# Two spreads of reciprocal sums per tile: from behind the transposes to behind the value products, one frame later

## The reference

```
x = x + 0.5 * ffn(layernorm(x))
x = x + attn(layernorm(x))
x = x + 0.5 * ffn(layernorm(x))
```

```
h = rmsnorm(x);  q, k, v = h @ qkv_w + qkv_b      # 16 query heads, 4 key heads, 64 wide; rotary
attn[h] = exp(q k' / 8 - logaddexp(logsumexp(q k' / 8), sink[h]))     # causal, window 128
x = x + concat_h(attn[h] @ v) @ proj_w + proj_b
h2 = rmsnorm(x);  4 of 32 experts per token by h2 @ gate_w;  x + sum_k w_k * expert_k(h2)
```

## Time and profile before

| | us |
|---|---|
| median of 3 runs (1331.86 to 1332.47) | 1332.41 |
| the profiled execution | 1331.51 |
| its span, first to last instruction | 1329.6 |
| TensorE busy (share of the span) | 1012.1 (76%) |
| VectorE busy | 827.7 (62%) |
| GpSimd busy | 649.6 (49%) |
| ScalarE busy | 565.6 (43%) |

### The profile page before, as it was taken

The page is one execution under the profiler, slowest core; times in us unless marked ns, Lnnn a source line. Parts: engine busy times, 40 slices in busy tenths (PEclk is TensorE's granted clock), DMA queues, the critical chain, the costliest instruction groups (busy, mean ns, idle before and its releaser), DMA issues.

```text
span 1329.6 us, 24766 instructions
## 1 busy us (share of the span) xinstructions
PE 1012.1 (76%) x7773; PEld 733.2 (55%) x7834; DVE 827.7 (62%) x2064; ACT 565.6 (43%) x2156; POOL 649.6 (49%) x860
## 2 busy tenths in 40 slices
PE   2899999999358854888888959999999990888100
PEld 1567666676347743555555536667666660777100
DVE  4788888886324422777777758898888761343121
ACT  0455555556223421555555616555555650444000
POOL 2234565564756225556553232466555545740575
PEclk9899999999769985899999979999999995899655
DMA  6677777766124320000000011233211101442221
GB/s 187 160 177 183 189 193 183 173 165 144 48 80 138 109 70 20 19 17 19 21 17 7 1 40 56 74 103 102 93 57 43 36 17 32 134 125 84 71 67 51
DMA packets 98779, 116.60 MB, mean 88 GB/s; under 512 B 14816, under 2 KB 73952, under 8 KB 98656
## 3 DMA queue, kind: packets, MB, share of 16 engines
q1 hardware_dynamic: 76688, 57.73, 13.8%
q10 hardware_dynamic: 10704, 34.21, 12.3%
q0 software_dynamic: 11264, 23.09, 6.2%
HBM read 38.37 MB, written 55.71 MB: 71 GB/s over the span
## 4 chain that ended last, share of the span: by engine, by line
PE 44%; DVE 10%; POOL 8%; issue 6%; POOLq 2%; ACT 2%; DMA 2%; DVEq 0%; SPq 0%; ACTq 0%
PE ps L911 6%; PE ps L819 6%; PE ps L801 5%; POOL shared L1690 4%; PE ps L930 4%; PE ps L706 4%; PE ps L774 3%; PE ps L836 3%; PE ps L740 2%; PE ps L922 2%; PE ps L847 2%; POOLq L474 2%; PE ps L901 2%; DVE shift L1081 2%; DVE pT L1086 1%
## 5 line engine op out<-in xcount | busy, mean ns | idle before, releaser
L1371 ACT ACTIVATE prob<-ps,shift 128x128 f32<-128x128 f32 (+1 forms) x768 | 312.5, 422 | 137.1 <-DVE shift L1081 136.1
L1081 DVE TENSOR_REDUCE shift<-ps 128x4 f32<-128x512 f32 (+1 forms) x192 | 182.6, 951 | 45.0 <-PE ps L803 19.8
L819 PE MATMUL ps<-tb,prob 128*128 128x128 f32 x1152 | 171.8, 285 | 0.1
L1086 DVE COPY pT<-ps 128x512 f32<-128x512 f32 x192 | 131.7, 686 | 46.3 <-PE ps L819 45.9
L819 PEld LDWEIGHTS ps<-tb,prob 128*128 128x128 f32 x1152 | 123.8, 142 | 64.4 <-issue 58.6
L1371 ACT ACTIVATION_READ_ACCUMULATOR prob<-ps,shift 128x1 f32 x768 | 158.7, 207 | 0.0
L1606 POOL DMA_INDIRECT routed<-row_out,row_at x128 | 130.7, 1021 | 26.3 <-issue 24.7
L1680 POOL DMA_INDIRECT qT<-routed,rows_at x96 | 91.7, 956 | 74.2 <-PE ps L901 29.0
L836 PE MATMUL ps<-pT,v 128*64 128x256 f32 x768 | 111.5, 395 | 17.2 <-issue 11.9
L774 PE MATMUL ps<-keyT,qT 64*128 64x256 f32 (+1 forms) x1024 | 119.7, 352 | 1.4 <-issue 1.4
L1398 ACT ACTIVATE yraw<-ps 128x256 f32<-128x256 f32 x128 | 49.2, 384 | 160.9 <-PE ps L836 160.3
(11 more groups left out here) (159 smaller groups left out, 1848.6 us busy)
## 6 DMA issues: line engine op xcount, KB each, us to landing
routed<-nothing ACTq DMA_DIRECT2D x16, 2048.0 KB, 12.7
swapped<-rot_b SPq DMA_DIRECT2D x160, 128.0 KB, 2.1
answers<-yraw SPq DMA_DIRECT2D x48, 256.0 KB, 2.3
shared<-in_w_up SPq DMA_DIRECT2D x32, 256.0 KB, 3.2
qT<-routed SPq DMA_DIRECT2D x96, 64.0 KB, 1.9
shared<-in_w_down SPq DMA_DIRECT2D x32, 128.0 KB, 3.4
routed<-row_out,row_at POOLq DMA_INDIRECT x128, 2.4
qT<-routed,rows_at POOLq DMA_INDIRECT x96, 2.7
```

What stands on the lines that cost most here:

```text
L819: last = pe.transpose(ps[:, BANK_SIDE + bank, h * P:(h + 1) * P], prob[:, s % 4, h, c * P:(c + 1) * P], ident)
L1081: dve.tensor_reduce(shift[:, lt % 2, 4 * g:4 * g + 4], score_view(L, s, lt), AX.X, ALU.max, negate=True)\
L1086: dve.tensor_copy(pT[:, s % 2, 0, :], ps[:, BANK_SIDE + L.turned[k, s][0][0], :]).then_inc(S["pT_ready"], 1)
L1371: last = act.activation(prob[:, s % 4, h, 0:keys(lt)], score_view(L, s, lt)[:, h, :], ACT.Exp, bias=shift[:, lt % 2, one:one + 1], accum_o ...
```

## The change

The two spreads of a feed-forward tile move from slot 4 lt + 6 to slot 4 lt + 7. They no longer stand among the frame's steps but in a list of their own, frame.spreads. TensorE issues that list between weigh and turn_probs. The planner gives its uses their banks at the same point. VectorE takes the list right behind copy_pT and ahead of the remaining steps; the other engines have nothing to do for a spread. The middle layer stays as it was.

```
     def __init__(self, now, steps, weigh):
         self.now, self.steps, self.weigh = now, steps, weigh
+        self.spreads = []
...
             for half in range(self.halves):
-                steps[4 * lt + (6 if ffn else 7)].append((0, "spread", self.halves * lt + half))
+                steps[4 * lt + 7].append((0, "spread", self.halves * lt + half))
...
             frame = Frame(now, [], None)
 
+            spreads = [what for what in todo if ffn and what[1][1] == "spread"]
+            todo = [what for what in todo if not (ffn and what[1][1] == "spread")]
             todo.sort(key=lambda what: (what[1][0] == 0, what[1][1] == "place"))
...
                     self.result[k, s // 4] = self.bank_for("result", ("yraw_ready", 4 * k + s // 4 + 1))
+            for k, step in spreads:
+                n = self.step(frame, k, step, n)
+                frame.spreads.append(frame.steps.pop())
             if frame.unit(lag):
...
                             weigh(k, s, use)
+                        take(L, frame.spreads, front_step, tail_step)
                         if frame.unit(L.lag):
                             k, s = frame.unit(L.lag)
                             turn_probs(k, s)
...
                             copy_pT(k, s)
+                        take(L, frame.spreads, front_step, tail_step)
                         take(L, frame.steps[1:], front_step, tail_step)
```

## The result

The changed kernel takes 1379.71 us (median of 4 runs, 1378.18 to 1382.25), the kernel before 1332.13 beside it (1331.54 to 1332.47): a ratio of 1.0359, with 1.0342 to 1.0377 as its 95% interval. The profiled execution is the one of 1378.18 us; its span is 1376.3, against 1329.6. Only the feed-forward stages have these 46.7 us. From its first mask product to the end of its last send the first stage went from 329.07 to 349.04 us, the second from 322.50 to 349.25: 20.0 + 26.75 = 46.7, all of the difference.

The account below looks back on a forecast made before the run. TensorE, the fullest engine at 76% of the span, bounds the kernel. Halts of 28.2 us a stage, 56.3 for two, less 2.3 for the reciprocals, give +54 on 1331.5: 1385 us; own range 1367 to 1403, whole 1345 to 1406.

Parts of the forecast that it names:

- (a): Fourth frame, tiles with spreads there: the rope waits for its bank until the preceding rope's cosines end, 0.55 us.
- (b): Fifth frame, after fourth-frame spreads: the rope waits for pT and the first yT to free its bank, 1.1 us.
- (c): Eighth frame: turn_x waits for the pT copy that the spreads used to cover, 1.3 us.
- (d): Eighth frame: the weighted sum behind turn_x waits for ScalarE's pT copy, 0.4 us.
- (e): Eighth frame: the gate waits after the transposes for pT and the first yT to free its bank, 1.6 us.
- (f): First frame, after the eighth frame's gate: the rope waits for the second yT, 0.3 us.
- (g): Next crowded frame: VectorE enters later against TensorE, delaying row maximum, exponentials and weighted sum, 0.3 us.
- the 1.9 counted as given back: End of each feed-forward stage: the last-but-two tile's placing product no longer stands behind spreads, so 1.9 us comes back.
- Half swallowed, 1357 us: Rival: other engines catch up during halts, so half the predicted sum remains, 1357 us; chance 0.22.
- Faster by relief of the crowded frame: Rival: relief of each period's seventh frame, 1.6 us, and an earlier place at stage end give 1312 us; chance 0.08.
- No change: Rival: the gate's new wait just replaces those at spread and place, fourth frames stay whole, 1331 us; chance 0.06.
- The clock: Rival: feed-forward stages' granted clock falls to 0.91, costing 25 us per stage on top of 1385, 1435 us; chance 0.08.

Follow-up runs that it names:

- The first experiment: Changed kernel with VectorE taking the spread multiplications ahead of copy_pT instead of behind it: 1334.06 us, 1.0031 of the kernel before.
- the experiment with the last two tiles: Kernel before with only tiles 2 and 3 of each feed-forward stage's last round moved, VectorE taking spreads ahead of copy_pT: 1325.14 us, 0.9960.

## Why the prediction came out right, step by step

The forecast was 1385 us by halts that hang on banks of spreads which VectorE releases behind copy_pT. The first experiment shows that cause: with the order on VectorE's queue exchanged the loss falls from 47.6 to 2.9 us. Its terms, in a regular period of the second stage ("idle" is the number in brackets of the row, "frame" what the frame grew by, without the spreads):

| step | predicted us | measured us |
|---|---|---|
| (a) fourth frame's rope behind the cosines | 0.55 | 0.53 idle |
| (b) fifth frame's rope behind yT | 1.1 | 0.80 idle, frame +1.08 |
| fourth-frame tile, in all | 1.65 | 1.58 |
| (c) turn_x behind the pT copy | 1.3 | 1.04 idle |
| (d) weighted sum behind ScalarE's pT copy | 0.4 | 0.40 idle |
| (e) gate behind yT | 1.6 | 1.38 idle |
| (c), (d) and (e) together | 3.3 | 2.82 idle, frame +3.2 |
| (f) rope behind the second yT | 0.3 | frame +0.22 |
| (g) VectorE late in the next crowded frame | 0.3 | none |
| won at spread and placing product | 1.6 | 1.8 (seventh frame) |
| eighth-frame tile, in all | 2.3 | 1.63 |

Idle time alone is too small a measure: the rows of a full stretch overlap, those on the two sides of a halt don't, and the eighth frame grew by 0.4 us more than its three idle times. By the frames the halts were sized right to 0.1 us. The eighth-frame tile cost less than predicted because (g) did not come and the relief was 0.2 us larger.

**By period.** Each stage has eight periods of eight frames. Predicted, and measured as the difference of the two traces, in us:

| period | 1 | 2 | 3 to 6, each | 7 | 8 to the last send | sum |
|---|---|---|---|---|---|---|
| predicted | 1.5 (first stage -0.8) | 3.4 | 3.95 | 3.95 | 3.5 | 28.2 (25.9) |
| second stage | 0.59 | 3.35 | 3.21 to 3.22 | 4.57 | 5.38 | 26.75 |
| first stage | 2.79 | 3.53 | 2.47, 1.76, 1.76, 0.98 | 2.99 | 3.70 | 20.0 |

The sum of 54 us for both stages stands against 46.7. In both stages the nearness is in part luck. In the second the regular period was sized a fifth too high (3.95 against 3.21), the end too low (3.5 against 5.38). In the first the periods 3 to 6 cost 8.8 us less than predicted, the first period 3.6 more.

**(g) was wrong.** The weighted sum of the seventh frame waited 0.29 us, less than before (0.51): with the spreads gone VectorE has less to do there.

**The end of a stage.** In the second stage the three projections waited 1.85, 1.64 and 2.07 us, where 2.0 each was predicted; the last tile's waited 0.88, which the prediction did not have, and the 1.9 counted as given back did not come, since GpSimd stood longer ahead of it, as the experiment with the last two tiles shows. A drop of the clock, below, falls there too. These come to more than the 1.9 us by which the end was sized too low, so part of them overlaps; which part is open.

**The mis-sized term is the first stage's eighth frame.** (c) and (d) were taken from frames of the second stage. TensorE in the first:

```profile
188.81 0.44 PE L702 MATMUL ps<-tb,hh 128*128 128x128 f32 x2 [0.17 <-DVE pT L1093]
...
190.24 1.08 PE L842 MATMUL ps<-pT,v 128*64 128x256 f32 x8
...
195.48 0.41 PE L753 MATMUL ps<-wf,h2T 128*128 128x32 f32 x2 [1.38 <-DVE yT L1133]
```

(e) is the same 1.38 us, but (c) is 0.17 and (d) nothing, so this frame takes 7.67 us instead of 9.02: 1.3 a period, over most of the regular ones. In that stage VectorE comes into the frame earlier: it copies pT at 188.06, as the frame begins (188.05), where in the second stage the copy began 0.90 us after. The last section has rows on this. The two stages looked alike in the table by stretch; the frames of both should have been read. The first stage's -2.3 for the reciprocals failed too: that wait is gone, but the weighted sum ahead of it waits 2.99 instead, since the same VectorE queue is late there.

One name in the prediction was wrong: its "one block of keys" belongs to the units transposed in the fourth frame, not to the tiles (lt 1 and 3) whose spreads land there. The frames and durations used were the right ones.

**The rivals.** Half swallowed, 1357 us: in the second stage it fell, since the regular halts stand there at their price but for (g); in the first it holds for (c) and (d). Faster by relief of the crowded frame: the relief came, 1.8 us a period, but in the changed kernel the eighth frame lost 3.2, and even with VectorE's order mended turn_x behind the bare pT copy takes it back (1.0031). Its second half, the end of a stage, is real and gives 0.9960 by itself. No change: refuted.

**The clock** did not fall as that rival has it, but it isn't untouched. In a regular period it stays at 1.00, the level of 2.4 GHz, in every frame, also in the eighth, where TensorE idles 2.82 of 9.02 us in pieces of at most 1.38. But four times in the two stages TensorE ran some 3.5 us at half of it, the level of 1.2 GHz, where the kernel before stayed at 1.00: at 67.4, 320, 1088 and 1132, each 0.9 to 1.4 us after a halt (of 2.99, 1.85, 1.78 and 2.07 us) had ended. Not each such halt did it (none behind the 1.85 at 1095.57 or the 2.07 at 355.91). Shorter halts can be followed by a drop too: in the run with the spreads in their old frame, three halts of 1.38 us in the first stage were followed, 0.6 to 0.8 us later (at 108.3, 190.2 and 272.2), by 3.4 us at half clock, and four such halts were not. TensorE around the last of the four drops in the changed kernel:

```profile
1131.07 2.58 PE L746 MATMUL ps<-wf,yT 128*128 128x128 f32 x16 [2.07 <-DVE yT L1133]
1133.58 1.98 PE L842 MATMUL ps<-pT,v 128*64 128x256 f32 x8
```

At full clock these take 2.02 and 1.08 us, so a drop costs some 1.5 to 1.7, four at most 6.8 of the 46.7 us. The prediction's sum had no such term; that rival had 50 us for it. By the section of the Trainium skill that was weighed ("TensorE: Matmul & The Clock Gate", "A second HAM failure mode: psum-queue depth-cycling") short idles between groups of matmuls make the clock swing: the trace of the changed kernel disagrees for the halts of the regular periods and agrees for four of the longer ones, that other run for three of the short ones. What decides it is open.

## What to carry to other kernels

When a product moves ahead of other work on its engine's queue, move its reader ahead of that work's reader on the other queue too: a shared bank is held until the reader's queue gets to it, not until the product is there. Before a crowded frame is relieved, ask which waits its work covers; here the spreads covered a copy, and without them that copy stands in the open. A move that loses in the steady state can still win at the end of a stage, so try it on the last tiles alone.

## What the hardware did unexpectedly

The same small multiplication took VectorE 0.33 or 2.22 us. It is of 128x128 numbers, from SBUF to SBUF with a scalar per row. Already in the kernel before, its twelve instructions took 3.68 us in the first feed-forward stage and 11.36 in the second (the second column of this view of that line alone is the busy time):

```profile
35.40:357.70 322.30, 3.68 (x12) 0.98 0.69 165
793.10:1115.70 322.60, 11.36 (x12) 0.97 0.19 62
```

After the change, VectorE and GpSimd in the second stage, and then the same stretch of the first:

```profile
913.87 2.61 DVE L1023 TENSOR_SCALAR hh<-xr,mv,rstd 128x128 f32<-128x128 f32 x2
```

```profile
913.53 1.09 POOL L1614 DMA_INDIRECT routed<-row_out,row_at  x1 [0.17 <-issue]
914.66 1.28 POOL L1533 TENSOR_TENSOR qT<-rot_a,swapped 128x512 f32<-128x512 f32 x1
```

```profile
183.78 1.39 DVE L1018 TENSOR_SCALAR xn<-xr,mv,rstd 128x128 f32<-128x128 f32 x2
185.09 0.59 DVE L1023 TENSOR_SCALAR hh<-xr,mv,rstd 128x128 f32<-128x128 f32 x2
```

```profile
183.56 1.26 POOL L1533 TENSOR_TENSOR qT<-rot_a,swapped 128x512 f32<-128x512 f32 x1
184.78 0.18 POOL L1571 TENSOR_TENSOR msq_eps<-msq,eps 128x1 f32<-128x1 f32 x1
```

In the second stage the first of the two multiplications runs 2.22 us, from 913.87 to 916.09, and GpSimd's big addition ends at 915.94. The indirect DMA ahead of the addition is not enough: in the kernel before, the first multiplication of a pair, beside such a DMA alone, took 0.34 us at 927.58, and the second, which met the addition, 2.22. In the first stage the addition lies some 1.5 us earlier against VectorE's work, beside xn, which takes 1.39 us for two (0.59 in the second stage), and hh has only small operations beside it. So a small VectorE instruction seems to wait for a large one on GpSimd; no run here takes that neighbour away, and why GpSimd's order differs between the stages was not tried. The Trainium skill ("SBUF — State Buffer", "SBUF: two separate sides") says that VectorE and GpSimd share one pair of ports, which a GpSimd instruction, or a VectorE one in a two-port mode or with two inputs from SBUF, holds for its whole time while the other waits. These rows agree with it as far as they go; whether the multiplication ran in such a mode no row shows.
